# Attention: windows and probabilities moved in whole rows, far edges added two heads at a time

## The reference

```python
idx = jnp.clip(pos[None, :] - pos[:, None], -MAX_REL, MAX_REL) + MAX_REL
rk2 = rel_k[idx]
rv2 = rel_v[idx]
attn1 = jnp.einsum('bhqd,bhkd->bhqk', q, k)
attn2 = jnp.einsum('bhqd,qkd->bhqk', q, rk2)
attn = jax.nn.softmax((attn1 + attn2) / scale, axis=-1)
w1 = jnp.einsum('bhqk,bhkd->bhqd', attn, v)
w2 = jnp.einsum('bhqk,qkd->bhqd', attn, rv2)
```

## Time and profile before

| | |
|---|---|
| median of 3 runs | 2891.89 us (2887.56 to 2893.48) |
| the profiled execution | 2888.88 us, span 2887.0 us |
| busy: PE, DVE, ACT, POOL | 2526.3, 1694.0, 1181.7, 1386.0 us |
| granted TensorE clock, mean | 0.960 |
| DMA | 408590 packets, 199.39 MB |
| of these under 512 B | 312990 packets |

### The profile page before, as it was taken

The page is one execution under the profiler, slowest core; times in us unless marked ns, Lnnn a source line. Parts: engine busy times, 40 slices in busy tenths (PEclk is TensorE's granted clock), DMA queues, the critical chain, the costliest instruction groups (busy, mean ns, idle before and its releaser), DMA issues.

```text
span 2887.0 us, 49785 instructions
## 1 busy us (share of the span) xinstructions
PE 2526.3 (88%) x14884; PEld 1708.2 (59%) x14884; DVE 1694.0 (59%) x3890; ACT 1181.7 (41%) x2089; POOL 1386.0 (48%) x1121
## 2 busy tenths in 40 slices
PE   3697899988998889988899889998899888998877
PEld 1365556655675656656566655665566565666545
DVE  5746653676446764476645765367644676456625
ACT  1237422382234732356233742338223472235511
POOL 2446443573445544464553745357344554436322
PEclk8699999998999999999999999999899999999989
DMA  8605200661007600274004720066100760027300
GB/s 246 139 1 120 64 1 8 130 144 33 1 19 150 145 1 1 59 152 103 1 8 94 152 62 1 8 132 145 30 1 19 156 139 1 1 66 147 78 0 7
DMA packets 408590, 199.39 MB, mean 69 GB/s; under 512 B 312990, under 2 KB 404406, under 8 KB 405302
## 3 DMA queue, kind: packets, MB, share of 16 engines
q1 hardware_dynamic: 375270, 190.61, 28.8%
q10 hardware_dynamic: 33024, 5.24, 1.7%
HBM read 120.76 MB, written 75.02 MB: 68 GB/s over the span
## 4 chain that ended last, share of the span: by engine, by line
PE 54%; DVE 13%; issue 9%; SPq 7%; DMA 6%; POOL 5%; ACT 4%; DVEq 0%; POOLq 0%; ACTq 0%
PE PS L1626 50%; PE PS L1629 4%; DMA arena<-bias_scr 4%; SPq L595 2%; POOL arena L782 2%; DVE PS L1402 1%; SPq L669 1%; SPq L580 1%; DVE arena L1330 1%; DMA q_scr<-arena 1%; POOL crs L431 1%; DVE arena L1319 1%; DMA prob_scr<-arena 1%; DVE cbn L1297 1%; ACT arena L1123 1%
## 5 line engine op out<-in xcount | busy, mean ns | idle before, releaser
L1626 PE MATMUL PS<-arena 128*17 128x128 f32 (+7 forms) x6656 | 728.1, 305 | 72.6 <-ACT arena L1116 52.9
L1626 PEld LDWEIGHTS PS<-arena 128*17 128x17 f32 (+2 forms) x6656 | 486.5, 121 | 262.3 <-issue 134.6
L1629 PE MATMUL PS<-ident,arena 128*128 128x128 f32 (+1 forms) x3312 | 512.8, 281 | 97.2 <-DVE arena L449 26.2
L1629 PEld LDWEIGHTS PS<-ident,arena 128*128 128x128 f32 (+1 forms) x3312 | 377.1, 142 | 283.2 <-issue 127.7
L431 POOL TENSOR_TENSOR crn<-crn,mhalf 128x8 f32<-128x8 f32 (+1 forms) x208 | 373.1, 1798 | 167.0 <-DVE crn L1311 165.6
L1402 DVE CUSTOM_DVE_ANT_0 PS<-PS,arena 128x512 f32<-128x512 f32 x512 | 343.7, 714 | 166.1 <-POOL arena L782 152.4
L1626 PE MATMUL PS<-cwk,arena 128*128 128x512 f32 (+1 forms) x832 | 407.3, 613 | 2.4 <-ACT arena L1009 2.4
L1116 ACT ACTIVATE arena<-PS,nmax 128x512 f32<-128x512 f32 x512 | 345.3, 695 | 101.9 <-DVE nmax L1402 81.7
L1004 ACT ACTIVATE arena<-PS 128x512 f32<-128x512 f32 (+1 forms) x208 | 124.3, 597 | 512.5 <-PE PS L1626 512.5
L1123 ACT ACTIVATE arena<-PS 128x512 f32<-128x512 f32 x384 | 232.4, 606 | 7.0 <-PE PS L1626 5.8
L1626 PEld LDWEIGHTS PS<-cwk,arena 128*128 128x128 f32 (+1 forms) x832 | 156.8, 194 | 128.4 <-issue 115.2
(11 more groups left out here) (163 smaller groups left out, 3709.5 us busy)
## 6 DMA issues: line engine op xcount, KB each, us to landing
prob_scr<-arena SPq DMA_DIRECT2D x256, 104.0 KB, 2.8
arena<-bias_scr SPq DMA_DIRECT2D x128, 168.0 KB, 3.6
q_scr<-arena SPq DMA_DIRECT2D x128, 128.0 KB
arena<-q_scr SPq DMA_DIRECT2D x128, 128.0 KB, 3.3
arena<-bias_scr SPq DMA_DIRECT2D x128, 104.0 KB, 3.5
arena<-k_scr SPq DMA_DIRECT2D x16, 768.0 KB, 11.9
arena<-prob_scr SPq DMA_DIRECT2D x128, 80.0 KB, 2.5
arena<-far_scr SPq DMA_DIRECT2D x16, 546.0 KB, 7.8
```

The lines of the kernel that those rows point to most:

```text
L1626: return pe.matmul(o, l, r, start=start, stop=stop, **kw)
L1629: return pe.transpose(o, i, ident[0:i.shape[0], 0:i.shape[0]])
```

## The change

Windows and stores of probabilities are each moved by one DMA of all 128 partitions and all 168 columns, in place of two of 64 partitions. The columns left of the second half's bands are therefore loaded (zeros) instead of being set by `margins`, whose memsets of them go, with the waits behind these. The far edges are added in two operations of two heads each, and DVE waits for each of the two before the bias of its first head. The counts in the waits follow.

```diff
-HP = 64
-HWIN = HP + BAND
@@ load_window
-                rows_of = bias_scr[t, g * HG:(g + 1) * HG, 0:128 * WIN].rearrange("h (p r) -> p h r", r=WIN)
-                for lo, c in ((0, 0), (HP, HP)):
-                    sp.dma_start(Wn[lo:lo + HP, (g % 2) * HG:(g % 2 + 1) * HG, c:WIN], rows_of[lo:lo + HP, :, c:WIN])\
-                        .then_inc(win_loaded[g % 2], 16)
+                sp.dma_start(Wn[:, (g % 2) * HG:(g % 2 + 1) * HG, 0:WIN],
+                             bias_scr[t, g * HG:(g + 1) * HG, 0:128 * WIN]
+                             .rearrange("h (p r) -> p h r", r=WIN)).then_inc(win_loaded[g % 2], 16)
@@ store_probs
-                    rows_of = prob_scr[t, g * HG:(g + 1) * HG, 0:128 * WIN].rearrange("h (p r) -> p h r", r=WIN)
-                    for lo in (0, HP):
-                        sp.dma_start(rows_of[lo:lo + HP, :, lo:lo + HWIN],
-                                     P[lo:lo + HP, (g % 2) * HG:(g % 2 + 1) * HG, t * 128 + lo:t * 128 + lo + HWIN])\
-                            .then_inc(p_stored[g % 2], 16)
+                    sp.dma_start(prob_scr[t, g * HG:(g + 1) * HG, 0:128 * WIN].rearrange("h (p r) -> p h r", r=WIN),
+                                 P[:, (g % 2) * HG:(g % 2 + 1) * HG, t * 128:t * 128 + WIN]).then_inc(p_stored[g % 2], 16)
@@ load_band, and so wherever p_stored or win_loaded is waited for
-                    sp.wait_ge(p_stored[g % 2], 32 * ((b * T + t) * 2 + g // 2 + 1) + 1)
+                    sp.wait_ge(p_stored[g % 2], 16 * ((b * T + t) * 2 + g // 2 + 1) + 1)
@@ make_far
-                pool.wait_ge(far_added, m + 1)
+                pool.wait_ge(far_added, m * 2 + 1)
@@ far_edge
-                edges = Wn[:, (g % 2) * HG:(g % 2 + 1) * HG, BAND:WIN]
-                pool.tensor_tensor(edges, edges, Eb, ALU.add).then_inc(far_added, 1)
+                for j in range(0, HG, 2):
+                    edges = Wn[:, (g % 2) * HG + j:(g % 2) * HG + j + 2, BAND:WIN]
+                    pool.tensor_tensor(edges, edges, Eb[:, j:j + 2, :], ALU.add).then_inc(far_added, 1)
@@ margins
-            def margins(nb, g):
+            def margins(g):
                 if g == 0:
                     pool.memset(Wz[:, 0:NFAR], 0.0).then_inc(margins_zero, 1)
                 pool.memset(Wn[:, g * HG:(g + 1) * HG, WIN:WP], 0.0).then_inc(margins_zero, 1)
-                pool.wait_ge(margins_zero, 5 * nb + (2 if g == 0 else 4) + 1)
-                pool.sem_inc(waits_alone, 1)
-                pool.memset(Wn[HP:128, g * HG:(g + 1) * HG, 0:HP], 0.0).then_inc(margins_zero, 1)
-                pool.wait_ge(margins_zero, 5 * nb + (3 if g == 0 else 5) + 1)
-                pool.sem_inc(waits_alone, 1)
@@ bias
-                    if j == 0:
-                        dve.wait_ge(far_added, tile * NG + g + 2)
+                    if j % 2 == 0:
+                        dve.wait_ge(far_added, tile * (H // 2) + h // 2 + 2)
```

More of the change, by code:

```diff
@@ L705, in batch @@
                 sp.sem_inc(waits_alone, 1)
-                sp.wait_ge(p_stored[1], 32 * T * 2 * (b + 1) + 1)
+                sp.wait_ge(p_stored[1], 16 * T * 2 * (b + 1) + 1)
                 sp.sem_inc(waits_alone, 1)
@@ L733, in _ @@
             for k in range(2):
-                sp.wait_ge(win_loaded[k], 32 * T * 2 * NB + 1)
+                sp.wait_ge(win_loaded[k], 16 * T * 2 * NB + 1)
             for g in range(NG):
@@ L778, in far_edge @@
                 pool.sem_inc(waits_alone, 1)
-                pool.wait_ge(win_loaded[g % 2], 32 * ((nb * T + t) * 2 + g // 2 + 1) + 1)
+                pool.wait_ge(win_loaded[g % 2], 16 * ((nb * T + t) * 2 + g // 2 + 1) + 1)
                 pool.sem_inc(waits_alone, 1)
-                edges = Wn[:, (g % 2) * HG:(g % 2 + 1) * HG, BAND:WIN]
-                pool.tensor_tensor(edges, edges, Eb, ALU.add).then_inc(far_added, 1)
+                for j in range(0, HG, 2):
+                    edges = Wn[:, (g % 2) * HG + j:(g % 2) * HG + j + 2, BAND:WIN]
+                    pool.tensor_tensor(edges, edges, Eb[:, j:j + 2, :], ALU.add).then_inc(far_added, 1)
             def key_rest(nb):
@@ L866, in _ @@
             pool.wait_ge(m_act, 4 + 1)
-            margins(0, 0)
-            margins(0, 1)
+            margins(0)
+            margins(1)
             pads(0)
@@ L969, in batch @@
                     pool.sem_inc(waits_alone, 1)
-                    margins(b + 1, 0)
+                    margins(0)
                 finish(3)
                 if not final:
-                    margins(b + 1, 1)
+                    margins(1)
                     make_far(b + 1, 0, 0)
@@ L1111, in exps @@
                         act.wait_ge(mass_mul, m)
-                        act.wait_ge(p_stored[g % 2], 32 * (tile * 2 + g // 2) + 1)
+                        act.wait_ge(p_stored[g % 2], 16 * (tile * 2 + g // 2) + 1)
                     if t == 0 and h == HG - 1:
@@ L1426, in attn_dve @@
                             edge_sum(t, h // HG)
-                dve.wait_ge(margins_zero, 5 * (b + 1) + 1)
+                dve.wait_ge(margins_zero, 3 * (b + 1) + 1)
                 dve.sem_inc(waits_alone, 1)
```

## The result

The kernel after takes 2821.79 us (median of 4 runs, 2818.37 to 2831.20), against 2892.68 us before (4 runs beside them): a ratio of 0.9763, 95% interval 0.9743 to 0.9784, so 71 us faster. The sign was forecast and the size was not: 30 us were, and the range ended at 2833. The profiled execution took 2818.37 us, its span 2815.9.

The account below looks back on a forecast made before the run. Bound: attention's loop of window load, far edge and bias, with SP's issues late. Per image 5.4 + 37.6 + 27.5 = 70.5 us against 74.2, so -3.7, -30 over 8 images: 2862 us; range 2833 to 2890.

Parts of the forecast that it names:

- The window loop: Attention: SP's window issue, flight, far edge and bias, over two groups; 11.12 us before, 8.8 us predicted in tiles 0 and 1.
- the lag: From the end of bias m-2 to SP's issue of window m: 1.65 us falls to 0.25, 0.7 us a period.
- The image's start: Two memsets of 0.31 us and their waits leave each image's end; priced at 0, or 0.6 us an image without cover.
- the chain TensorE, ACT, TensorE: Attention: what is late next once SP is early, at 4.68 us a period; the eight periods were set to 4.70.
- the last six periods: Groups 9 to 15 of an image: a third of the far edge's 0.27 us credited, 4.68 to 4.58 us a period.
- no gain and no loss: The window's flight: 4.25 us in two halves, 4.2 us undivided; ends 3.6 and 4.9.
- The single issue: SP's one DMA issue in place of two: 0.63 us, saving 1.26 us a group; SP's round 4.88 to 3.62 us.
- The added bytes: Window and probability rows grow from 416 to 672 B: 0.6 us more of all 16 DMA engines a group, hidden if transfers fit.
- A: Rival, chance 0.12: the floor is lower, the loop's 4.4 us holds in all periods; -7.2 us an image, 2834 us.
- B: Rival, chance 0.12: the DMA takes half back, flight 4.2 + 1.0 us; -1.9 us an image, 2877 us.
- C: Rival, chance 0.08: slower, the DMA engines become the bound, long rows costing twice the price; 2907 us.
- D: Rival, chance 0.08: SP's issue of twice the rows costs twice as long, so nothing is removed; no change, 2892 us.

Follow-up runs that it names:

- split_only: The kernel before with the far edges added in two operations of two heads, DMAs unchanged; ratio 0.9952 to the kernel before.
- rows_only: The kernel after with the far edges again added in one operation of four heads; ratio 0.9824 to the kernel before.
- halves_whole_rows: The kernel after with each window and each store in two DMAs of 64 partitions, all 168 columns; ratio 1.0006 to the kernel before.
- no_window_loads: The kernel after without 14 of an image's 16 window loads, POOL waiting for the bias instead; ratio 0.9675 to the kernel before.
- pairs_same_waits: The kernel after with each window and store in two DMAs of two heads over all 128 partitions, same waits; ratio 0.9832 to the kernel before.

## Why the prediction was wrong

**What held.** The window loop was the bound, and SP's lateness a part of it. In the middle periods the lag became 0.21 us (0.25 was said); from SP's issue to the edge 4.43 (4.36); from the edge to bias 0.99, with two operations of 0.73 (0.95); the loop 8.95 (8.8). The image's start gave nothing: from the last group to the next image's first it is 268.5 us before and 268.4 after.

**The step that failed** is "What is late next is the chain TensorE, ACT, TensorE, whose pace with an early SP shows in the last six periods, 4.68". It made a floor of a stretch that was itself the loop. The rows said so: 0.25 + 4.36 of the earlier trace rows, the 1.55 from 627.71 to bias, and 3.26 of bias are 9.4 us for two groups, 4.7 a period, which is the measured 4.68. A pace that a loop explains is no sign of a second bound. `split_only`, which touches nothing but this loop, took it to 4.50 on the mean of the images (4.64 before), `rows_only` to 4.29, both to 4.13, and the floor is 4.10.

**A second step failed with it.** The window's flight was put at "no gain and no loss", so whole rows were worth nothing in tiles 2 and 3. They shortened the flight there from 4.06 to 3.45 us (`rows_only`) and took the lag from 0.35 to 0.18: 0.35 of the last six periods' 0.51. In tiles 0 and 1 the flight fell by 0.25 to 0.3. The lag, for its part, was read from one loop as 1.65 us and taken as the rule; the mean was 0.84, so SP's lateness was worth 0.63 us a loop and not 1.4.

On those means the last six periods gained 0.51 instead of the 0.06 that I credited, 2.7 us an image, and the middle ones 0.67 instead of 0.47, 1.6 us: 4.3 x 8 = 34 of the 41 us missed. Another 3 are the first period, which I kept at 5.4 of image 1 where the mean is 5.0. The last 4 lie outside these periods: 3 before the first bias of all (230.9 us, then 228.1), 1 behind the last. The former is 227.0 to 232.5 in the other runs, so it can't be put down to the change.

**Two more terms.** The single issue costs 0.36 us, not 0.63; SP's round loses 2 x (1.26 - 0.36) = 1.8 us instead of 1.26. The added bytes I priced at 0.6 us of the 16 engines a group, and the page of the kernel after has half of that (queue: packets, MB, share of 16 engines):
```profile
q1 hardware_dynamic: 371174, 215.76, 30.8%
```
30.8% of 2815.9 against 28.8% of 2887.0 us is 36 us more over 128 groups, 0.28 each. But this is the sum of two effects. `halves_whole_rows` has the rows of after and the form of before; against `split_only` (29.4% of 2875.1 us) it takes 95 us more, 0.74 a group. So the price of the bytes was about right, and what I put at nothing is the form: whole DMAs give 0.57 of it back (32.4% of 2900.9 us, then 30.8% of 2815.9). These differences are good to about 0.1, by which `split_only` and the kernel before differ with the same DMAs. By the size of 512 B in the Trainium skill (DMA: Bandwidth & Descriptors, Specifications), as the prediction reads it, the longer rows would cost no more. These runs don't bear that out. The packet records show no step at 512 B either: the medians are 18 ns for 256 B, 24 for 416, 27 for 512 and 33 for 672 (kernel before).

**The rivals.** A, the lower floor, is what happened: it had 2834 and 0.12, and was itself short, since it took the loop's 4.4 as the least; in tiles 2 and 3 the loop is 8.23 us, 4.12 a period. B and C did not happen: the flight fell instead of growing by 1 us, although the DMA share reached 0.89, over my 0.85. What this share costs isn't shown; at most it is the 0.4 us between the middle periods of after and of `no_window_loads`, whose share there is 0.63. D is refuted by the issue's 360 ns. The Trainium skill (DMA: Bandwidth & Descriptors, Rules for kernel authors) advises against two transfers to disjoint halves of the partitions, since both run on the same DMA engines, and to use one of 128. The advice is right here. But two DMAs of two heads over all 128 partitions share these engines just as well, and cost 0.7% where the halves cost 2.4; the other 1.7 lie in the form, with 608 ns of SP an issue and a slower transfer.

## What to carry to other kernels

Before a stretch is taken as the pace of "all the rest", add up the loop that you mean to cut in that same stretch: if the loop explains it and no link of it has slack, there is no floor yet. Count a queue that issues DMAs as an engine: here its 4.9 us of issues in a 5.2 us period (the round shown) were in no busy share. Read a wait or a lag from many loops before it is priced: the one shown had twice the mean. When a DMA like these is cut in two, cut it so that each part keeps all 128 partitions, and expect a split of the first operation after a wait to pay less where what comes before the wait is late.

## What the runs showed of the hardware

The duration of a window's DMA issue on SP went by the partitions that it covers and not by its rows: medians of 608 ns over 64 partitions and 360 over 128, for 256 rows and for 512. Back to back, two over 128 partitions have a median of 462 (`pairs_same_waits`). The stores of probabilities go the same way (596 in the kernel before, 360 after), but not every DMA does: the band stores of 128 partitions (L510 of the kernel after) have a median of 617 and a least of 359. I had expected more rows to take longer, if anything.

The transfer was slower in halves as well: with the same rows, 46.0 ns a row of 672 B against 40.6 (means). Why an issue or a row takes longer in that form, no run shows.
